# Scattering the attention scores inside the projection: the last graph attention of a four-layer network on Trainium2

## What is computed

```python
def _L3_gnn_ref(x, edge_index, W, att_src, att_dst, bias, gamma, beta):
    xh = (x @ W).reshape(N, H, D)
    a_src = jnp.einsum('nhd,hd->nh', xh, att_src)
    a_dst = jnp.einsum('nhd,hd->nh', xh, att_dst)
    ...
    e = jax.nn.leaky_relu(a_src[src] + a_dst[dst], NEG_SLOPE)
    m = jax.ops.segment_max(e, dst, num_segments=N)
    e = jnp.exp(e - m[dst])
    denom = jax.ops.segment_sum(e, dst, num_segments=N)
    alpha = e / denom[dst]
    msg = xh[src] * alpha[:, :, None]
    out = jax.ops.segment_sum(msg, dst, num_segments=N).reshape(N, H * D) + bias
```

## Time and profile before

| | us |
|---|---|
| runs shown, median (3) | 5703.5 |
| lowest, highest | 5690.11, 5710.98 |
| the profiled execution's own time | 5698.39 |
| its span, first to last instruction | 5696.6 |
| p3, from its opening to SP's value store | 4440.7 to 4485.41 |
| starts stage, from SP's first load to the attention's first load | 4500.92 to 4551.91 |

### The profile page before, as it was taken

How to read it: one execution, slowest core, us unless ns; L and a number is a source line. 1 busy time by engine, 2 the same in 40 slices (tenths; PEclk the granted TensorE clock), 3 DMA queues, 4 the chain that set the end, 5 groups by cost and what they waited for, 6 DMA issues and landing times. The chain is left out here.

```text
span 5696.6 us, 81178 instructions
## 1 busy us (share of the span) xinstructions
PE 4330.3 (76%) x22765; PEld 3321.6 (58%) x22765; DVE 2719.3 (48%) x6033; ACT 1748.5 (31%) x4277; POOL 2470.6 (43%) x2520
## 2 busy tenths in 40 slices
PE   7884298799999819995889889249999277771297
PEld 6662277688888606663677677137777166661254
DVE  8886384689889650001343333142111445544622
ACT  5561031133333202210455455113333123330121
POOL 0275576555555257775445444300000277773000
PEclk6686599999999858997999999678999678886577
DMA  1174265799999630001455454210000167773000
GB/s 37 53 225 132 77 206 183 248 306 309 307 306 309 202 92 16 17 16 47 121 137 132 126 137 124 71 45 1 0 0 0 53 176 199 197 198 116 11 0 23
DMA packets 589572, 705.53 MB, mean 124 GB/s; under 512 B 139536, under 2 KB 515512, under 8 KB 588856
## 3 DMA queue, kind: packets, MB, share of 16 engines
q0 software_dynamic: 118624, 306.99, 18.5%
q1 hardware_dynamic: 304146, 222.19, 13.6%
q10 hardware_dynamic: 166630, 174.25, 9.8%
HBM read 446.09 MB, written 257.12 MB: 123 GB/s over the span
## 5 line engine op out<-in xcount | busy, mean ns | idle before, releaser
L1681 POOL DMA_INDIRECT a_far<-kv_table,a_index x416 | 464.9, 1118 | 438.1 <-DVE a_index L1848 337.2
L2300 POOL DMA_INDIRECT fl_far<-x_table,fl_index x416 | 415.1, 998 | 449.9 <-DVEq L2469 325.2
L2001 POOL DMA_INDIRECT a_far<-src_table,a_index x416 | 450.5, 1083 | 131.9 <-issue 124.4
L1191 POOL DMA_INDIRECT by_dst<-dst_row,place x416 | 409.3, 984 | 211.2 <-issue 109.5
L1191 POOL DMA_INDIRECT by_src<-src_row,place x416 | 407.7, 980 | 161.4 <-issue 114.8
L2360 PE MATMUL ps<-fl_w,fl_hid 128*128 128x256 f32 x1664 | 452.8, 397 | 0.0
L1708 PE MATMUL ps<-a_w,a_edge_t 128*128 128x256 f32 x1664 | 395.3, 381 | 0.0
L2226 POOL DMA_INDIRECT starts_opening<-dst_table,starts_key_i x4 | 4.3, 1068 | 844.1 <-DMA starts<-starts_zero 843.2
L2360 PEld LDWEIGHTS ps<-fl_w,fl_hid 128*128 128x128 f32 x1664 | 322.9, 200 | 48.6 <-issue 3.9
L2492 DVE TENSOR_TENSOR fl_msg<-ps,fl_far 128x256 f32<-128x256 f32 x416 | 176.0, 423 | 365.3 <-PE ps L2360 365.3
L229 PE MATMUL ps<-const_sb,xn_sb 128*128 128x128 f32 x350 | 58.5, 338 | 376.9 <-DVE xn_sb L218 376.9
(11 more groups left out here) (482 smaller groups left out, 9930.1 us busy)
## 6 DMA issues: line engine op xcount, KB each, us to landing
partial<-a_out ACTq DMA_DIRECT2D x208, 546.0 KB, 5.9
a_edge<-by_dst SPq DMA_DIRECT2D x104, 516.0 KB
partial_f<-fl_out ACTq DMA_DIRECT2D x26, 2056.0 KB, 9.7
dst_row<-in_edge_attr SPq DMA_DIRECT2D x52, 1024.0 KB
xn_sb<-q_table SPq DMA_DIRECT2D x416, 128.0 KB
f_w<-in_L_ffn_W SPq DMA_DIRECT2D x4, 2048.0 KB
by_dst<-dst_row,place POOLq DMA_INDIRECT x416
a_far<-kv_table,a_index POOLq DMA_INDIRECT x416
```

Of the source, the lines that this page charges most:

```text
L1191: self.nc.gpsimd.indirect_dma_start(out=self.table, out_offset=bass.IndirectOffsetOnAxis(ap=self.place[:, n:n + 1], axis=0), in_=self.row[ ...
L1681: gathered[b % 4].count(nc.gpsimd.indirect_dma_start(out=far[:, b, u, :], out_offset=None, in_=kv_table, in_offset=bass.IndirectOffsetOnAx ...
L2001: gathered[b].count(nc.gpsimd.indirect_dma_start(out=far[:, b, u, :], out_offset=None, in_=src_table, in_offset=bass.IndirectOffsetOnAxis( ...
L2300: gathered[q].count(nc.gpsimd.indirect_dma_start(out=far[:, q, t, :], out_offset=None, in_=table, in_offset=bass.IndirectOffsetOnAxis(ap=i ...
```

## The change

`starts_stage` is gone and its work is part of `project3_stage`:

- `near` is scattered straight from on-chip memory, without the reload. POOL waits for each tile's `bank_free` and scatters it (lines 2866 and 2867 of the changed kernel), 25 in all, and after them waits for the store of `dst_table` and makes the four gathers.
- SP loads the keys and stores the zeros at the stage's opening. It stores the value rows in five parts, each when its five tiles are done; before the fifth it stores `near`.
- VectorE clears `zero`, makes the indices and casts the keys before its first tile.
- The stage has ten semaphores, where p3 had five and the starts stage six. One barrier is gone.

The computation is the same.

```diff
-def starts_stage(core, base, count, by_dst, node_rows, table):
...
+def project3_stage(core, xt, early, src_table, dst_table, base, count, by_dst, starts):
...
             @block.sync
             def _(sp):
-                sp.wait_ge(bank_free, TILES + GROUP)
-                sp.dma_start(src_table.rearrange("(a p) d -> p a d", p=P), out[:]).then_inc(stored, 16)
-                sp.dma_start(dst_table.rearrange("(a p) d -> p a d", p=P), near[:]).then_inc(stored, 16)
-                sp.wait_ge(stored, 32)
+                sp.dma_start(key[:], by_dst.rearrange("(q p r) w -> p q r w", q=4, r=P)[:, :, 0, D:D + 1], allow_slow_non_contiguous=True).then_inc(key_loaded, 16)
+                sp.wait_ge(zeroed, 1)
+                sp.dma_start(starts.rearrange("p t w -> p (t w)"), zero[:]).then_inc(cleared, 16)
+                for g in range(GROUPS):
+                    sp.wait_ge(bank_free, GROUP * (g + 1) + GROUP)
+                    if g == GROUPS - 1:
+                        sp.dma_start(dst_table.rearrange("(a p) d -> p a d", p=P), near[:]).then_inc(near_stored, 16)
+                    sp.dma_start(src_table[g * GTOK:(g + 1) * GTOK, :].rearrange("(a p) d -> p a d", p=P), out[:, g * GROUP:(g + 1) * GROUP]).then_inc(stored, 16)
+
+                gathered.wait(sp, 4 * 16)
+                scattered.wait(sp, TILES * 16)
+                sp.dma_start(starts[0].rearrange("(q p) w -> p q w", q=4), opening[:]).then_inc(stored, 16)
+                sp.wait_ge(stored, 16 * GROUPS + 16)
+
+            @block.gpsimd
+            def _(pool):
+                pool.wait_ge(indexed, 1)
+                pool.wait_ge(cleared, 16)
+                for a in range(TILES):
+                    pool.wait_ge(bank_free, a + 1 + GROUP)
+                    scattered.count(nc.gpsimd.indirect_dma_start(out=flat, out_offset=bass.IndirectOffsetOnAxis(ap=at[:, 2, a:a + 1], axis=0),
+                                                 in_=near[:, a, :], in_offset=None,
+                                                 bounds_check=EPAD - 1, oob_is_err=False))
+                pool.wait_ge(near_stored, 16)
+                for q in range(4):
+                    gathered.count(nc.gpsimd.indirect_dma_start(out=opening[:, q, :], out_offset=None, in_=dst_table,
...
             @block.vector
             def _(dve):
                 ch = Chain(dve, chain)
+                nc.vector.memset(zero[:], 0.0).then_inc(zeroed, 1)
...
+                ch.link(nc.vector.tensor_copy(at[:, 2], f[:, 2]))
+                dve.wait_ge(key_loaded, 16)
+                ch.link(nc.vector.tensor_copy(key_i[:], key[:, :, 0]))
+                dve.sem_inc(indexed, 1)
                 dve.wait_ge(loaded, 48)
```

More of the change, by code:

```diff
@@ L2172, in _ @@
                 run(dve, MSG, quarter, lambda: ch.loop(BODIES - 2, 2 * (1 + 4 + 2)))
-def starts_stage(core, base, count, by_dst, node_rows, table):
[L2178 to L2226, removed]
-                                                 in_offset=bass.IndirectOffsetOnAxis(ap=key_i[:, q:q + 1], axis=0),
-                                                 bounds_check=NPAD - 1, oob_is_err=False))
-                for a in range(TILES):
-                    scattered.count(nc.gpsimd.indirect_dma_start(out=flat, out_offset=bass.IndirectOffsetOnAxis(ap=at[:, 2, a:a + 1], axis=0),
-                                                 in_=own[:, a, :], in_offset=None,
-                                                 bounds_check=EPAD - 1, oob_is_err=False))
@@ L2894, in project3_stage @@
         prod = st.sb("prod", [P, 2, D])
-        chain, projected, bank_free, copied, stored = (st.sem(s) for s in ("chain", "projected", "bank_free", "copied", "stored"))
+        zero = st.sb("zero", [P, ETILES * HEADS])
+        f = st.sb("f", [P, 3, TILES])
+        at = st.sb("at", [P, 3, TILES], I32)
+        key, key_i = st.sb("key", [QT, 4, 1]), st.sb("key_i", [QT, 4], I32)
+        opening = st.sb("opening", [QT, 4, HEADS])
+        chain, projected, bank_free, copied, near_stored, stored = (st.sem(s) for s in ("chain", "projected", "bank_free", "copied", "near_stored", "stored"))
+        key_loaded, zeroed, cleared, indexed = (st.sem(s) for s in ("key_loaded", "zeroed", "cleared", "indexed"))
+        gathered, scattered = st.moved(0, 4), st.moved(1, TILES)
+        flat = starts.rearrange("p t w -> (p t) w")
         with st.block() as block:
@@ L3010, in gnn_ffn_kernel @@
                 src_table, dst_table = dram("src_table", (NPAD, SEG)), dram("dst_table", (NPAD, HEADS))
-                project3_stage(core, xt, early, src_table, dst_table)
-        starts = dram("starts", (P, ETILES, HEADS))
-        starts_stage(core, base, count, by_dst, dst_table, starts)
+                starts = dram("starts", (P, ETILES, HEADS))
+                project3_stage(core, xt, early, src_table, dst_table, base, count, by_dst, starts)
         attend3_stage(core, ends, src_table, starts, partial)
```

10 lines of the change are left out of this document (9 added, 1 removed).

## The result

| | before | changed |
|---|---|---|
| median | 5700.9 us (6 runs, 5690.1 to 5711.0) | 5649.6 us (6 runs, 5646.2 to 5661.8) |
| ratio | | 0.9913, 95% interval 0.9898 to 0.9929 |
| profiled execution | 5698.4 us | 5653.7 us |
| first matmul of p3 to the attention's first load | 110.85 us | 61.46 us |

The account below looks back on a forecast made before the run. VectorE paced the projection; 66.5 us without tensor computation then preceded the POOL-bound attention. Its first load moving from 4551.91 to 4502.2 gains 49.7 us, taking the profiled 5698.4 to 5648.7; forecast 5651, range 5637 to 5671.

Parts of the forecast that it names:

- The head: Projection's opening: VectorE's clear, indices and key cast come first, so the first product is 2.4 us later.
- The caution about the key load: Projection's opening: if the key load took the zero store's 5.4 us to land, it would add 0.5.
- The scatters: Projection: POOL catches up after some five tiles, then follows each tile; all 25 scatters, 31.9 us, leave the path.
- it does not overlap: Rival: POOL let go only at the projection's end; gain of 22 us, 5679 us; chance 0.05.
- The score store: After the last tile: issued ahead of the last fifth of the values, it lands in 4.2 us, bounds 2.0 and 14.1.
- The end: Behind the score store: four gathers, opening store and stage's end; attention's first load at 4502.2 against 4551.91.
- About 16 to 17 us: Sign to look for in the new profile: time from the last tile to the attention's first load.
- has 14 us: Stage's end: the last value part would be late if its cover went, but has 14 us.
- The attention: Last attention: POOL's; starting earlier, it ends as much earlier, its 416 gathers 450 us busy as before.
- VectorE's hold on POOL: Rival: VectorE's products stretch every scatter to 1.52 us; 5654 us, or 5667 at twice that excess; chance 0.05.
- The slow score store: Rival: the score store still takes 14.1 us, so the chain ends 9.9 later, 5661 us; chance 0.08.
- the moved code: Rival: code moved in memory stalls POOL in each of the last attention's 13 rounds, 27 us lost, 5678; chance 0.02.

Follow-up runs that it names:

- e9: Changed kernel with VectorE clearing 416 columns that the zero store reads eight times, key cast between fifth and sixth tile; first matmul to attention's first load 58.86 us.
- e4: Changed kernel with POOL held until the projection's end before its first scatter; first matmul to attention's first load 89.74 us.
- e8: Changed kernel with the scores too stored in five parts, each ahead of its value part; first matmul to attention's first load 59.66 us.
- e3: Changed kernel with one value store after the last tile and the score store behind it; first matmul to attention's first load 71.45 us.
- e6: Changed kernel without the opening rows: no four gathers, no opening store; first matmul to attention's first load 54.46 us.
- e10: Changed kernel with the projection's products reading values from on-chip memory instead of PSUM; first matmul to attention's first load 61.45 us.
- e5: Kernel before with values stored in five parts, scores ahead of the fifth, starts stage kept; first matmul to attention's first load 102.58 us.
- e7: Changed kernel with GpSimd clearing the zeros and the key cast between VectorE's fifth and sixth tile; first matmul to attention's first load 61.18 us.
- e2: Changed kernel with the score store behind the fifth value part; first matmul to attention's first load 63.64 us.
- e1: Changed kernel with one value store after the last tile, behind the score store; first matmul to attention's first load 64.39 us.

## Why the prediction was right

Forecast 5651 with a range of 5637 to 5671 (5651 - 13 is 5638; the lower end is off by 1), measured 5649.6. That the whole time came within 1.4 us is closer than such a measurement can bear out, as its interval alone is 18 us wide. The stretch allows a check of each step rather than of the sum alone.

1. **The head.** The forecast was 2.4 us later; it was 2.9 (5.24 - 2.34 after the first matmul). The clear began 0.78 us after SyncE's first issue, not 0.4, and 0.22 us lie between the key's cast and the product, where I had 0.1. The caution about the key load was needless: issued with nothing in front of it, it took 0.33 us instead of 2.09 and had landed in time. e9, which takes most of the clear off the path and moves the cast behind the fifth tile, returns 2.6 of it.
2. **The scatters.** Six at about 1.3 us, then 1.68 apart, the last at 0.97 us beside the score store: as forecast (25 x 1.28 is 32.0, where the forecast has 31.9). The landing of the zero store (5.4) was as forecast. That they hide behind the tiles and not behind something else is shown by e4, which loses 28.3 us when they may not. It is also the rival "it does not overlap", priced at a gain of 22; it gains 21.1.
3. **The score store.** Forecast 4.2 from issue to landing, bounds 2.0 and 14.1; measured 3.8. The term was built from the packets' 2.0 and a small transfer's 2.2. Its sum held, its split did not: e8, without four fifths of the packets, lands 1.9 us earlier, where 2.0 for all of them would make it 1.6. If the time goes straight by the count, 3200 packets are 2.4 us and the rest 1.4, an estimate from 3.8 and 1.9. One part was too small and the other too large, and they nearly cancelled. The upper bound belongs to the order, not to the transfer: in e3, with the full value store in front, the scores landed 13.3 us after their issue.
4. **The end.** From the score store's issue to the attention's first load the forecast's own steps give 14.4 us (4487.8 to 4502.2), and 14.2 were measured. "About 16 to 17 us" in the list of what would show it did not follow from those steps; it was a slip there, and the sum did not use it. The claim that the fifth value part "has 14 us" was too generous: e6 puts its slack at 7. It still wasn't on the path.
5. **The attention** starts earlier and ends as much earlier, apart from 6.1 us in the profiled execution. They come out of the gathers' spread, that is, of how often a gather starts under a product (see e10); e5 has the old starts stage and 457.6 us busy. The forecast had it at 450 us as before.

The head took 0.5 more than forecast, the end 0.2 less; that is the 0.3 between 49.7 and 49.4. Of the rivals, VectorE's hold on POOL is settled by the durations of 0.97, and e10 bounds it for products on chip. The rival's price of 1.52 us for every scatter was taken from one gather beside a product of 1.22 us; by what e10's section found, a product of 0.42 can hold a scatter by 0.29 at most, an estimate from 0.42 and 0.13. The slow score store did not come true (3.8). And no gather of the attention waits more than 0.3 us for its issue, so the moved code costs nothing here.

Where the 49.4 us come from, by the runs: 28.3 are the overlap (e4). The other 21.1 can be read in e4 against before. There the stores' tail (4485.41 to 4500.92, 15.5 us) and the head of the starts stage with its loads, clear, indices and zero store (4500.92 to 4510.85, 9.9) have left the path, together 25.4. Against that stand the 2.9 that VectorE pays at the head, 0.9 of release from the last tile to the first scatter, and 0.5 in the gathers and the closing stores. That the stores' tail really leaves hangs on their order and parts: with the old order and one value store 10.0 of it stay (e3).

## What to carry to other kernels

A short stage between two long ones costs its whole latency, whatever its share of busy time. If its inputs are made tile by tile on chip, look for the engine that idles in the stage before and let it follow each tile; the test is whether it is faster per tile (1.28 us) than the one that it follows (1.68). In one queue put the small transfer that a chain waits for ahead of the large one that only has to be done, and price small packets by their count. Before moving a clear from VectorE to GpSimd, look at what VectorE does at that moment.

## What the runs showed of the hardware that was not expected

- GpSimd's clear of 3328 columns (2.87 us) held one small cast on VectorE until it ended: 0.12 us became 2.86 (e7).
- A gather or scatter of GpSimd that starts while a VectorE product with both inputs on chip is running is held: its duration is 1.00 us plus what is left of the product less 0.13, within 0.02 us, for the 76 and 83 gathers of the last attention in before and after that start with 0.13 to 1.2 us left. One that starts first is not held by the product (0.97 for the fourth scatter of e10), apart from ten gathers of before that start 0.50 to 0.58 us ahead of a product and take up to 1.13.
- How long an issue on SyncE takes depends on what is queued in front of it. The score store's took 0.36 us with nothing new ahead of it, 0.53 behind a 660 KB value part (e2), 5.45 behind 3300 KB (e3). A value part took 1.57 behind 3200 small packets and 0.53 behind 640 (e8).
- 100 KB in 3200 packets landed 3.8 us after the issue, 20 KB in 640 packets 1.9.
- One chip ran the same programs a fifth slower (before: 6880 us against 5701), while the stretch's instructions kept their durations. Part of the extra time is in instruction issue: gaps that POOL's gathers put down to it came to 226 us in the last attention of e1, against 124 in the trace of after. The granted TensorE clock was lower too, 0.78 in e1 against 0.84, and TensorE was busy 4524 us against 4345. How much of the extra time each of these is, and what makes that chip slow, was not tried.
